# Cross-attention chain on one core: the mask load, the key and value units and the probability transposes of the audio block in another order

## What is computed

```python
# x: (8, 56, 256); ctx: (8, 1500, 256); mask: (8, 1500), all true
for i in (1, 2):                                  # L0, 16 heads of 128, one extra bias key/value
    h = layer_norm(x)
    q, k, v = heads(h @ wq + bq), heads(ctx @ wk + bk), heads(ctx @ wv + bv)
    p = softmax(q @ [k; bias_k].T / sqrt(128))    # (8, 16, 56, 1501)
    x = x + (p @ [v; bias_v]) @ wo + bo
x = x + gelu(layer_norm(x) @ w_fc1 + b_fc1) @ w_fc2 + b_fc2
# L1, 16 heads of 16
kv = layer_norm(ctx) * gamma + beta
q, k, v = heads(x @ Wq), heads(kv @ Wk), heads(kv @ Wv)
s = q @ k.T / sqrt(16);  s = where(mask, s, -big)
x = x + tanh(gate) * (softmax(s) @ v) @ Wo
```

## Time and profile before

| | us |
|---|---|
| median of 3 runs | 1571.32 (1569.82 to 1574.19) |
| the profiled execution, whole | 1565.11 |
| its span in the profile | 1563.4 |
| PE busy | 1436.4 (92% of the span) |
| DVE busy | 1024.7 (66%) |
| ACT busy | 833.2 (53%) |
| POOL busy | 479.2 (31%) |
| granted PE clock, mean over the execution | 0.976 |

### The profile page before, as it was taken

How to read it: one execution, slowest core, us unless ns; L and a number is a source line. 1 busy time by engine, 2 the same in 40 slices (tenths; PEclk the granted TensorE clock), 3 DMA queues, 4 the chain that set the end, 5 groups by cost and what they waited for, 6 DMA issues and landing times.

```text
span 1563.4 us, 24187 instructions
## 1 busy us (share of the span) xinstructions
PE 1436.4 (92%) x9106; PEld 883.0 (56%) x9106; DVE 1024.7 (66%) x2150; ACT 833.2 (53%) x1437; POOL 479.2 (31%) x459
## 2 busy tenths in 40 slices
PE   7889999999999989899999999999988888889876
PEld 3356666666666533566666666665444444444444
DVE  6755555555556557666666666656568878888885
ACT  4544444555545446454545554445446766667663
POOL 5523334233333100433342333300016344542300
PEclk8999999999999989999999999999999999999998
DMA  6188888888989510798898888876117998998886
GB/s 208 40 186 184 169 178 179 180 170 180 186 164 177 153 55 14 175 185 172 180 187 163 180 179 178 170 152 186 51 41 157 181 173 179 189 207 173 155 158 122
DMA packets 665392, 246.84 MB, mean 158 GB/s; under 512 B 638028, under 2 KB 639548, under 8 KB 665276
## 3 DMA queue, kind: packets, MB, share of 16 engines
q1 hardware_dynamic: 665276, 245.30, 75.2%
HBM read 85.28 MB, written 0.52 MB: 55 GB/s over the span
## 4 chain that ended last, share of the span: by engine, by line
PE 77%; DVE 11%; DMA 5%; ACT 3%; SPq 2%; issue 1%; POOL 0%; ACTq 0%; POOLq 0%; DVEq 0%
PE SC L710 43%; PE PV L710 34%; DVE prob L1402 3%; DVE qc L1420 2%; DVE core L1459 2%; SPq L523 2%; DMA mask<-in_mask_dram 2%; DMA core<-core 2%; DMA core<-qc 1%; DVE core L1309 1%; ACT rowbuf L1183 1%; DVE core L1451 1%; ACT qc L1178 0%; DVE prob L1314 0%; DVE qc L1328 0%
## 5 line engine op out<-in xcount | busy, mean ns | idle before, releaser
L710 PE MATMUL PV<-core 128*128 128x256 f16 (+1 forms) x4800 | 543.7, 272 | 31.9 <-issue 9.7
L710 PEld LDWEIGHTS PV<-core 128*128 128x128 f16 x4800 | 462.4, 98 | 102.6 <-issue 19.2
L1113 ACT ACTIVATE prob<-SC,nmax 128x500 f32<-128x500 f32 x336 | 223.7, 674 | 429.4 <-DVE nmax L1426 429.4
L710 PE MATMUL SC<-ctxT,qc 128*128 128x500 f16 x2016 | 443.1, 374 | 2.6 <-DVE qc L1328 2.6
L1395 DVE TENSOR_REDUCE mx<-SC 128x1 f32<-128x500 f32 x336 | 224.6, 669 | 324.7 <-PE SC L710 324.7
L710 PEld LDWEIGHTS SC<-ctxT,qc 128*128 128x128 f16 x2016 | 195.5, 97 | 210.0 <-DVE qc L1328 3.5
L1451 DVE SCALAR_TENSOR_TENSOR core<-prob,core 128x1500 f16<-128x1500 f32 x112 | 197.2, 1761 | 9.3 <-ACT core L1122 9.3
L643 POOL CAST ctxT<-stage 128x750 f16<-128x750 f32 x64 | 53.6, 838 | 479.5 <-PE SC L710 240.9
L1122 ACT ACTIVATE core<-prob 128x1500 f16<-128x1500 f32 x112 | 162.7, 1453 | 3.5
L710 PE MATMUL SC<-qc 128*128 128x512 f16 x480 | 122.2, 402 | 40.8 <-DVE mx L1402 40.8
L710 PE MATMUL SC<-ctxT 128*128 128x512 f16 x576 | 140.0, 388 | 14.9 <-DVE core L1459 14.8
(11 more groups left out here) (141 smaller groups left out, 1337.7 us busy)
## 6 DMA issues: line engine op xcount, KB each, us to landing
stage<-in_ctx_nat_dram SPq DMA_DIRECT2D x64, 384.0 KB, 3.8
stage<-in_ctx_t_dram SPq DMA_DIRECT2D x64, 375.0 KB, 3.3
stage<-in_ctx_p_dram SPq DMA_DIRECT2D x32, 384.0 KB, 3.7
core<-in_wq_dram SPq DMA_DIRECT2D x8, 512.0 KB, 3.7
core<-in_wk_dram SPq DMA_DIRECT2D x8, 512.0 KB, 3.6
core<-in_wv_dram SPq DMA_DIRECT2D x8, 512.0 KB, 4.7
core<-in_wo_dram SPq DMA_DIRECT2D x8, 512.0 KB, 5.4
qc<-core SPq DMA_TRANSPOSE x144, 2.5
```

Source lines behind the costliest of these rows:

```text
L710: return nc.tensor.matmul(o, a, c, start=start, stop=stop, skip_group_check=skip)
L1113: nc.scalar.activation(prob[:, i, c * CW:c * CW + w], SETS[i][c][:, 0:w], ACT.Exp, bias=nmax[:, i, :], accum_out=sum3[:, i, c:c + 1]).then ...
```

## The change

The tables of the order, the time of the mask's steps, the way the probabilities are turned, and the sign of the scores. The SBUF for three more value places comes from small tensors that move into a part of `core` that is not yet in use when they are needed. One DVE instruction of each tile is gone, the negation of the maximum: the scores are now made with the opposite sign, and their minimum serves as it stands. The core of the diff:

```diff
-VSLOTS = 30
+VSLOTS = 33
-        LN_UNITS = [[0], [1], [2], [3, 4]]
-        MLP_UNITS = [5, 6, 7, 8, 9, 10, 11]
-        SLOT_UNITS = [(0, 1, 2), (3, 4), (5, 6, 7), (8, 9), (10, 11), (), ()]
-        SLOT_KEYS = {2: 0, 3: 1, 4: 2, 5: 3}
-        SLOT_WINDOWS = {1: (-1, 2), 2: (-1, 3), 5: (0, 0), 6: (0, 1)}
-        SLOT_PICKS = {0: (-1, 1), 2: (-1, 2), 3: (-1, 3), 6: (0, 0)}
+        LN_UNITS = [[0, 1], [2, 3], [4, 5], [6, 7, 8]]
+        MLP_UNITS = [9, 10, 11, 12, 13, 14, 15]
+        PRE_UNITS = NT + 4
+        SLOT_UNITS = [(4, 5), (6,), (7, 8), (9, 10), (11,), (NT, NT + 1), (NT + 2, NT + 3)]
+        SLOT_KEYS = {0: 0, 2: 1, 4: 2, 5: 3}
+        SLOT_WINDOWS = {1: (-1, 2), 2: (-1, 3), 4: (0, 0), 6: (0, 1)}
+        SLOT_PICKS = {0: (-1, 1), 2: (-1, 2), 3: (-1, 3), 5: (0, 0)}
...
             def turn_probs(t):
-                sp.wait_ge(ph_lo, t + 1)
+                sp.wait_ge(ph_hi, t + 1)
                 if t >= 2:
                     sp.wait_ge(pv_done, t - 1)
-                sp.dma_start_transpose(pT[:, i, :, :], ph[:, i, :]).then_inc(pt_full[i], 16)
+                sp.dma_start_transpose(pT[:, i, 0:NT, :], ph[:, i, 0:TC]).then_inc(pth_full[i], 16)
+                sp.wait_ge(ph_lo, t + 1)
+                sp.dma_start_transpose(pT[:, i, NT:2 * NT, :], ph[:, i, TC:2 * TC]).then_inc(ptl_full[i], 16)
...
             def turn_audio(y):
-                sp.wait_ge(aph_lo, y + 1)
+                sp.wait_ge(aph_hi, y + 1)
...
-                sp.dma_start_transpose(probT[:, :, s * P:(s + 1) * P], aph[:, i, :]).then_inc(apt_full[i], 16)
+                sp.dma_start_transpose(probT[:, 0:NT, s * P:(s + 1) * P], aph[:, i, 0:TC]).then_inc(apth_full[i], 16)
+                sp.wait_ge(aph_lo, y + 1)
+                sp.dma_start_transpose(probT[:, NT:2 * NT, s * P:(s + 1) * P], aph[:, i, TC:2 * TC])\
+                    .then_inc(aptl_full[i], 16)
...
-                if s == 4 and b + 1 < B:
+                if s == 1 and b + 1 < B:
                     mask_load(b + 1)
...
             def weigh(l, x):
-                pe.wait_ge(pt_full[i], 16 * (t // 2 + 1))
+                pe.wait_ge(pth_full[i], 16 * (t // 2 + 1))
...
                 for j in range(NT):
                     w = width(j)
-                    for n, (pi, ci) in enumerate(((0, 0), (1, 0), (0, 1))):
-                        ins = mm(PV[i][:, 0:D], pT[0:w, i, pi * NT + j, :], nat[0:w, par, ci, j, :],
-                                 j == 0 and n == 0, j == NT - 1 and n == 2)
+                    for ci in range(2):
+                        mm(PV[i][:, 0:D], pT[0:w, i, j, :], nat[0:w, par, ci, j, :], j == 0 and ci == 0, False)
+                pe.wait_ge(ptl_full[i], 16 * (t // 2 + 1))
+                for j in range(NT):
+                    w = width(j)
+                    ins = mm(PV[i][:, 0:D], pT[0:w, i, NT + j, :], nat[0:w, par, 0, j, :], False, j == NT - 1)
...
             def audio_scores(y):
-                if s == 0:
-                    for i in range(2):
-                        pe.wait_ge(kt_full[i], 16 * PIECES // 2 * (b + 1))
...
                 for c in range(NB):
+                    if s == 0:
+                        for k in range(c, c + 2):
+                            pe.wait_ge(kt_full[k % 2], 16 * (PIECES // 2 * b + k // 2 + 1))
...
             def audio_average(b, w):
-                for i in range(2):
-                    pe.wait_ge(apt_full[i], 16 * ((y + 2 - i) // 2))
...
-                for j in range(NT):
-                    r = width(j)
-                    for i in range(2):
+                for i in range(2):
+                    for k in range(2):
+                        pe.wait_ge((apth_full, aptl_full)[i][k], 16 * ((y + 2 - k) // 2))
+                    for j in range(NT):
+                        r = width(j)
...
             def audio_exponentiate(y):
-                act.wait_ge(as_negmax, y + 1)
-                nc.scalar.activation(prob[:, i, 0:T], prob[:, i, 0:T], ACT.Exp, bias=nmax[:, i, :],
+                act.wait_ge(as_max, y + 1)
+                nc.scalar.activation(prob[:, i, 0:T], prob[:, i, 0:T], ACT.Exp, scale=-1.0, bias=mx3[:, i, 0:1],
...
             def audio_attention():                     # ACT
-                        mask_row(b + 1, (b + 1) % 2)
+                    if s == 3 and b + 1 < B:
+                        mask_row(b + 1, (b + 1) % 2)
                     if s == 5 and b + 1 < B:
                         mask_addend(b + 1, (b + 1) % 2)
...
-            def audio_maximum(y):
+            def audio_minimum(y):
-                    op0=ALU.add, op1=ALU.max, accum_out=mx3[:, i, 0:1]).then_inc(as_max, 1)
-                dve.wait_ge(as_max, y + 1)
-                nc.vector.tensor_scalar(nmax[:, i, :], mx3[:, i, 0:1], -1.0, None, ALU.mult).then_inc(as_negmax, 1)
+                    op0=ALU.add, op1=ALU.min, accum_out=mx3[:, i, 0:1]).then_inc(as_max, 1)
...
             def audio_low(y):                          # and the same in probs_low, with ptl_full
                 dve.wait_ge(aph_hi, y + 1)
+                if y >= 2:
+                    dve.wait_ge(aptl_full[i], 16 * (y // 2))
...
             def audio_attention():                     # DVE
-                    for j in last[0:1]:
-                        unit_low(NT * (b + 1) + j, y)
                     if 0 < y <= RT * B:
                         audio_low(y - 1)
-                    for j in last[1:]:
-                        unit_low(NT * (b + 1) + j, y)
+                    for n in slot_units(y - 1)[1:]:
+                        unit_low(n, y)
...
-                    if s == 5 and b + 1 < B:
+                    if s == 4 and b + 1 < B:
                         mask_term_of(b + 1)
```

More of the change, by code:

```diff
@@ L125, in build @@
         at += P
+        stt = core[:, at:at + 2 * B * NT].rearrange("p (i n) -> p i n", i=2)
+        at += 2 * B * NT
+        ptokc = core[:, at:at + TILES]
+        at += TILES
+        bkd = core[:, at:at + 2 * H].rearrange("p (l h) -> p l h", l=2)
+        at += 2 * H
+        bkd16 = core[:, at:at + 2 * H].bitcast(F16).rearrange("p (l s h) -> p l s h", l=2, s=2)
+        at += 2 * H
+        hm8 = core[:, at:at + 2 * HW]
+        at += 2 * HW
+        vbias = core[0:WC, at:at + NW]
+        at += NW
+        rsum = core[:, at:at + 4].rearrange("p (i n) -> p i n", i=2)
+        at += 4
+        nmax = core[:, at:at + 2].rearrange("p (i n) -> p i n", i=2)
+        at += 2
         assert at <= (VSLOTS + KSLOTS) * UNIT // 2
@@ L237, in build @@
         aph_lo = sem("aph_lo")
-        apt_full = [sem(f"apt_full{k}") for k in range(2)]
+        apth_full = [sem(f"apth_full{k}") for k in range(2)]
+        aptl_full = [sem(f"aptl_full{k}") for k in range(2)]
         apv_done = sem("apv_done")
@@ L294, in build @@
         ph_lo = sem("ph_lo")
-        pt_full = [sem(f"pt_full{k}") for k in range(2)]
+        pth_full = [sem(f"pth_full{k}") for k in range(2)]
+        ptl_full = [sem(f"ptl_full{k}") for k in range(2)]
         av_hi = sem("av_hi")
@@ L371, in build, with slot_units @@
         HEAD_KV = {1: 0, 2: 1, 3: 2, 4: 3, 5: 4}
-        LN_UNITS = [[0], [1], [2], [3, 4]]
-        MLP_UNITS = [5, 6, 7, 8, 9, 10, 11]
-        SLOT_UNITS = [(0, 1, 2), (3, 4), (5, 6, 7), (8, 9), (10, 11), (), ()]
-        SLOT_KEYS = {2: 0, 3: 1, 4: 2, 5: 3}
-        SLOT_WINDOWS = {1: (-1, 2), 2: (-1, 3), 5: (0, 0), 6: (0, 1)}
-        SLOT_PICKS = {0: (-1, 1), 2: (-1, 2), 3: (-1, 3), 6: (0, 0)}
+        LN_UNITS = [[0, 1], [2, 3], [4, 5], [6, 7, 8]]
[5 more added lines that the diff above has]
+        SLOT_PICKS = {0: (-1, 1), 2: (-1, 2), 3: (-1, 3), 5: (0, 0)}
+        def slot_units(y):
+            b, s = divmod(y, RT)
+            return [NT * (b + 1) + j for j in SLOT_UNITS[s] if 0 <= y and NT * (b + 1) + j < NT * B]
         def at_slot(table, y):
@@ L849, in unit @@
                     pe.wait_ge(kv_lo, DC)
-                if n < NT and n >= 2:
+                if n < PRE_UNITS and n >= 2:
                     pe.wait_ge(m_lo, n - 1)
-                if n == NT:
-                    pe.wait_ge(m_lo, NT)
+                if n == PRE_UNITS:
+                    pe.wait_ge(m_lo, PRE_UNITS)
                     pe.wait_ge(aq_lo, NW)
-                if n >= NT + NB:
+                if n >= PRE_UNITS + NB:
                     pe.wait_ge(m_lo, n - 2)
@@ L905, in audio_attention @@
                 for y in range(RT * B + 3):
-                    b, s = divmod(y, RT)
-                    if b < B:
+                    if y < RT * B:
                         audio_scores(y)
-                    if b + 1 < B:
-                        for j in SLOT_UNITS[s][0:1]:
-                            unit(NT * (b + 1) + j, y)
+                    for n in slot_units(y)[0:1]:
+                        unit(n, y)
                     if at_slot(SLOT_WINDOWS, y):
                         audio_average(*at_slot(SLOT_WINDOWS, y))
-                    if b + 1 < B:
-                        for j in SLOT_UNITS[s][1:]:
```

(20 more changed lines are left out.)

40 lines of the change are left out of this document (19 added, 21 removed).

## The result

The kernel after takes 1500.5 us in the median of four runs (1496.2 to 1503.5), the kernel before 1570.6 beside it: a ratio of 0.9558, 95% interval 0.9536 to 0.958, so 70 us or 4.4% faster. The forecast was 1516, the range 1500 to 1546. The profiled execution took 1499.85 us (span 1497.9), 65.3 less than that of before.

A forecast was written before the change was run, and what follows sets the result against it. The audio block was taken as a DVE-PE-ACT loop with one long mask stop per batch, DVE bounding it afterwards. Batches 45.0, end 5, L0 12, minus 6.4 ahead gave 55.6 us gained: 1516 us, range 1500 to 1546.

The forecast's parts named there:

- Mask steps: Audio block: DVE's 3.49 us stall for the mask goes, 7 times; PE's clock loss of up to 1.75 us not counted.
- Negation: Audio block: 56 DVE instructions of 0.154 us go, 1.1 us per batch, and exponentials start that much sooner.
- Units in all slots: Audio block: with one or two units per slot, a walk through the slots gives DVE about 40.5 us per batch.
- Half transposes: Probability transposes: two halves take no more SP or DMA time than a whole; high half issued about 1.8 us earlier.
- Rival B: L0 attentions and audio block: a half transpose costs more than half a whole, so slower, about 1595 us; chance 0.05.
- 42.0 us per middle batch: Audio block, batches 1 to 5: 40.5 us of DVE plus 1.5 for waits on landings; bounds 40.5 and 45.5.
- Rival A: Audio block: the DMA queue sets the pace, a middle batch takes 45.5 us, total 1546 us; chance 0.20.
- Ends of L0: L0 layers: shorter waits at the first `weigh` and the layers' ends gain 12 us (8 to 16).
- Four units ahead: Before the audio block: four more units cost 6.4 us (5 to 7.5), with PE held about 2 us before unit 8.
- End of the audio block: Last batch and tail: slots without units, and shorter transpose waits and landings, gain 5 us (3 to 6).
- Rival C: Audio block: stops only change place, the batch stays at 47.5 us or so, total about 1571 us; chance 0.05.

The follow-up runs named there:

- the extra DMA: Kernel after with one more DMA per slot, SP writing 384 KB of a weight tile to an unread scratch tensor: 1561.2 us, ratio 0.9958.
- gate: Kernel after with POOL waiting for DVE's lower half of slot 4 before it splits the third piece: 1500.2 us, ratio 0.9555.
- multiply: Kernel after with the small multiply by 4096 moved from DVE to ACT: 1501.1 us, ratio 0.956.
- unit 8: Kernel after with unit 8 moved from ahead of the MLP to behind its second hidden block: 1499.7 us, ratio 0.9557.

## Why the prediction was right, and where it was off

**Total.** 1500.5 against 1516, and half a microsecond inside the lower end of the range. The sign, the order of the parts and most sizes hold. Of the 15 us missed, 9.9 are in the terms, by the table at the top: 5 x 1.0 in batches 1 to 5, 1.9 in batch 0, 2.2 in batch 6, the last one and the tail together, 1.6 ahead of the loop, less 0.8 in L0. The rest is mostly the difference between the profiled executions (65.3 gained), for which the sum was made, and the medians (70.0).

**Mask steps.** Right: 3.49 us of stall, 3.5 us per batch measured alone. The 1.75 us that the forecast saw overlapped as loss of clock don't come on top.

**Negation.** Forecast 1.1 us per batch. With such an instruction back, the middle batch is 0.4 longer, but in an execution in which the lower halves were 1.0 us per batch shorter (1871 instead of 2016 ns each). The 1.1 us of DVE's time is there; what the negation is worth alone isn't shown.

**Units in all slots.** The step's walk gave 40.5 us of DVE per batch, and DVE is busy 40.2 to 40.5. But the text also said 38.6 to 39, and that is what the same instructions would take undisturbed: 35 lower halves at 0.25 us over their 1.77 are 8.6 us, 1.7 per batch. The walk was right by luck: its gaps between instructions were taken by a collision that it didn't have. The step gave no price of its own to the tables. The runs show one, and that it depends on the rest: 10 us alone, 33 to 37 as the last part in.

**Half transposes.** The step held that in the middle batches they bring nothing but room. They bring 9 us (taken back) to 12 (alone) in the loop. Alone, it is the waits of ACT and PE for whole transposes, 18 us in five batches, and the mask's load, which comes earlier on SP. Taken back, 6.4 of the 9 us lie in the middle batches, and there it is mostly DVE's collisions with POOL, by the table above; that halves avoid these in general isn't shown. That the halves need no more time in L0 holds: a tile still takes 7.75 us with 224 halves (three starts of `weigh` at 307.23, 314.99 and 322.75), and L0 ended at 1106.0 us in the mean of ten kernels with halves, 1117.6 in that of four with whole ones, before among them. Rival B is refuted. The 336 us that the prediction worked out from the Trainium skill, "DMA: Bandwidth & Descriptors", for a price that nothing hides, do not show either: 168 more transfers went with a gain. That doesn't contradict the page, which calls the 2 us mostly completion latency; they and bytes/436e3 stand in its section Anatomy of one DMA, not in Bandwidth, which has the advice on 1 MiB.

**42.0 us per middle batch.** The term that was most mis-sized: 41.0. The 1.5 us for landings on top of DVE were not needed: ACT waits for none, and DVE is idle for 0.8 us per batch in all.

**Rival A.** Refuted as stated, with a share of 1 as the ceiling and 45.5 us per batch: 1.12 is carried over whole batches. Something of it is left, as the extra DMA shows, but how much, and whether it is the engines or the queue, stays open. The prediction's estimate of 39.3 us for the batch's 8.9 MB at 226 GB/s isn't tested either: the 217 GB/s of the kernel after are just these bytes over its 41 us.

**Ends of L0.** Forecast 12; by the means above 11.6. The wait of about 1 us is there (1.03).

**Four units ahead.** Forecast -6.4, measured -5; the mechanism as said, a wait for the bank of unit 6 (3.10 us, not 2). The 2.6 us for a unit at half rate were not there: the granted clock was 1.00 in the first 14 us of the stretch in the profiled execution. It was 0.76 and 0.75 in the two executions that took 3 and 5 us more. What was not foreseen is that avoiding the wait wins nothing.

**End of the audio block.** Forecast 5 with the last batch; 4.1 after the last minimum and 3.2 in the last batch (30.2 to 27.0).

**Rival C.** Refuted for the change as a whole. But three of the follow-ups (gate, multiply, unit 8) won nothing that can be told from the scatter.

## What to carry to other kernels

A table that spreads work over slots is worth little while stalls fill the slots, and much when they are gone; so measure a part by taking it away from the full version too, not only by adding it to the old one. Once an engine is busy for nearly the whole batch, add up its busy time before and after each further step: moving one instruction can change how long the others take. A trace in which only POOL waits for DMA doesn't say that there is room for more of it. When a wait is taken away on one queue, look at what else stood behind it there: the mask's load came earlier through the transposes.

## What the runs showed of the hardware

DVE's instruction with two SBUF inputs of 1500 columns takes 1.77 us alone and 2.6 to 3.2 us when POOL's subtract with two SBUF inputs (1.65 us) starts up to 0.7 us ahead of it; the minimum, with one input in PSUM, kept its 1.71 us where the next subtract (1235.86 to 1237.50) ran across its start at 1236.49. The Trainium skill, "SBUF — State Buffer", section Who interferes with whom, says that DVE and GpSimd share a pair of ports with an exclusive lock, and that a DVE instruction with two SBUF inputs contends with a GpSimd instruction that reads SBUF. The trace agrees: started at 1230.93, behind a subtract that ends at 1232.55, the lower half would end at 1234.32 if it waited it out; it ended at 1234.13. So do all nine lower halves in the middle batches of the kernel after that start during a subtract: each ends 0.19 or 0.20 us before the subtract's end plus 1.77.

A DMA share above 1 is carried for long: 1.12 over batches of 41 us, at 216 to 217 GB/s with transposes, 1.11 at 235 GB/s with plain writes among them.
